# Two layers of attention on one core: the second attention's value products issued in bursts of four key blocks into a projection bank, with six score banks, three row slots, eight probability units and another order of the queues

## The reference, cut to what matters

```python
xn = _layernorm(x); x = x + L0_attn(xn) + L0_ffn(xn)     # 16 heads of 64, ALiBi slopes, causal
xn = _layernorm(x); x = x + L1_attn(xn) + L1_ffn(xn)     # 8 heads, differential, rotary

# L0_attn:  softmax(q k^T * SCALE + rel * slope, causal) @ v, then @ w_out + b_out
# L1_attn:  for each of 8 heads two score sets (q1,k1), (q2,k2) of width 8, no mask
o1 = sdpa(q1, k1, vfull); o2 = sdpa(q2, k2, vfull)       # vfull is 16 wide
o  = o1 - lam * o2
o  = o * rsqrt(mean(o*o) + EPS) * ln_w + ln_b
out = (o * (1 - LAMBDA_INIT)).reshape(b, s, e) @ Wo.T
# ffn:  z = silu(h @ w1 + b1) @ w2 + b2 ;  residual + 0.5 * z   (w1, w2 dequantised)
```

## Time and profile before

| | |
|---|---|
| three runs | 2512.21 us median (2510.09 to 2514.51) |
| the profiled execution's own time | 2513.58 us |
| its span, first to last instruction | 2511.6 us |
| TensorE busy / weight loads | 2370.6 us (94%) / 1112.7 us (44%) |
| DVE / ACT / POOL busy | 1856.1 (74%) / 1882.8 (75%) / 1430.7 us (57%) |
| mean granted TensorE clock | 0.986 |

### The profile page before, as it was taken

One profiled execution on the slowest core, in us unless ns is written; L12 is line 12 of the kernel. 1 busy time (PEld: TensorE's weight loads), 2 busy tenths in 40 slices (PEclk: granted clock), 3 DMA queues, 4 the chain that ended last, 5 costly groups with the idle time before them and its releaser, 6 DMA issues.

```text
span 2511.6 us, 81917 instructions
## 1 busy us (share of the span) xinstructions
PE 2370.6 (94%) x32896; PEld 1112.7 (44%) x32896; DVE 1856.1 (74%) x5637; ACT 1882.8 (75%) x4707; POOL 1430.7 (57%) x1356
## 2 busy tenths in 40 slices
PE   6999999999999999999999999999999999999886
PEld 2454444444444444444444444444444444444421
DVE  4558777777877778777777877778777776867675
ACT  4866787878778777787878778777787878778545
POOL 5866474665656556474665656556574655646311
PEclk8999999999999999999999999999999999999978
DMA  3002020200202002020200202002020200202020
GB/s 96 7 14 45 3 61 3 49 15 7 57 2 57 6 19 44 3 61 3 53 10 7 56 3 61 3 21 43 7 56 3 55 8 7 57 3 56 2 56 5
DMA packets 59944, 70.43 MB, mean 28 GB/s; under 512 B 11056, under 2 KB 55344, under 8 KB 56368
## 3 DMA queue, kind: packets, MB, share of 16 engines
q1 hardware_dynamic: 59568, 65.21, 11.5%
HBM read 35.04 MB, written 29.36 MB: 26 GB/s over the span
## 4 chain that ended last, share of the span: by engine, by line
PE 72%; ACT 14%; DVE 10%; issue 2%; DMA 1%; POOL 1%; SPq 0%; POOLq 0%; ACTq 0%; DVEq 0%
PE pj L1436 17%; PE pj L1532 10%; PE sc L1500 9%; PE op L1561 7%; PE sc L1517 7%; ACT pt L989 5%; PE pj L1548 5%; PE pj L1456 5%; DVE mx L1250 4%; PE sc L1605 4%; PE sc L1591 4%; ACT pq L949 3%; ACT pt L967 3%; PE pj L1426 3%; DVE pq L1197 2%
## 5 line engine op out<-in xcount | busy, mean ns | idle before, releaser
L818 POOL TENSOR_SCALAR pq<-pq,rsum 128x128 f32<-128x128 f32 (+3 forms) x1024 | 1130.5, 1121 | 743.0 <-DVE rsum L1204 742.6
L1250 DVE TENSOR_REDUCE mx<-sc 128x1 f32<-128x512 f32 x1024 | 655.9, 683 | 199.1 <-PE sc L1605 195.1
L989 ACT ACTIVATE pt<-sc 128x512 f32<-128x512 f32 x1024 | 556.3, 610 | 191.5 <-PE sc L1591 191.2
L949 ACT ACTIVATE pq<-pq,mx 128x128 f32<-128x128 f32 (+3 forms) x1024 | 573.2, 576 | 16.6 <-DVE mx L1197 16.6
L967 ACT ACTIVATE pt<-sc 128x512 f32<-128x512 f32 (+1 forms) x768 | 360.8, 538 | 221.2 <-PE sc L1517 217.7
L1197 DVE CUSTOM_DVE_ANT_0 pq<-sc,relkey 128x128 f32<-128x128 f32 (+3 forms) x1024 | 448.3, 484 | 104.9 <-PE sc L1500 100.0
L1500 PE MATMUL sc<-K,Q 64*128 64x128 f32 (+3 forms) x2048 | 365.5, 454 | 26.9 <-ACT pt L989 16.7
L1532 PE MATMUL pj<-pt,v 128*32 128x512 f32 (+3 forms) x4096 | 304.5, 438 | 3.9 <-ACT y L917 0.6
L1517 PEld LDWEIGHTS sc<-ident,pq 64*128 64x128 f32 x5120 | 199.2, 139 | 171.6 <-issue 127.3
L1436 PE MATMUL pj<-xnT,wqkv 128*32 128x512 f32 x2048 | 264.4, 609 | 7.6 <-DVE xres L1173 2.9
L1561 PE MATMUL op<-pt,v 128*32 128x512 f32 x1920 | 256.8, 607 | 2.2 <-ACT pt L989 2.0
(11 more groups left out here) (117 smaller groups left out, 2798.2 us busy)
## 6 DMA issues: line engine op xcount, KB each, us to landing
scr_p<-y SPq DMA_DIRECT2D x160, 128.0 KB, 2.4
QS<-scr_p SPq DMA_DIRECT2D x30, 384.0 KB, 6.1
KS<-scr_p SPq DMA_DIRECT2D x30, 384.0 KB, 8.8
x_in<-in_L_attn_x SPq DMA_DIRECT2D x16, 256.0 KB, 2.8
scr_p<-tanh SPq DMA_DIRECT2D x32, 128.0 KB, 2.4
out_x<-xres SPq DMA_DIRECT2D x15, 256.0 KB, 2.3
QS<-nrow SPq DMA_DIRECT2D x180, 4.0 KB
wqkv<-in_L_attn_w_qkv SPq DMA_DIRECT2D x1, 1536.0 KB, 6.5
```

What stands on the lines that cost most here:

```text
L818: pool.tensor_scalar(rows, rows, rsum[:, p % NROWS, c:c + 1], None, ALU.mult).then_inc(s_scl, 1)
L949: act.activation(rows, rows, ACT.Exp, scale=-1.0, bias=mx0[:, p % NROWS, c:c + 1], accum_out=lsum[:, p % NROWS, c:c + 1]).then_inc(s_exp0, 1)
L989: act.activation(pt1[:, GS * (m % 2) + 2 * j + h, :], sc[tile_bank(i, "st1", 2 * n + h)][:, :], ACT.Exp, scale=float(DS) ** -0.25).then_in ...
L1250: dve.reduce_max(mx1[:, g % 2, at:at + 1], sc[tile_bank(i, "mx1", 2 * t + h)][:, :], AXIS.X).then_inc(s_mxd1, 1)
```

## The change

It has five parts.

1. `pv1` is called once for a group instead of four times: 16 matmuls in a row, over the four key blocks, each block behind its own wait for the exponentials. Its result goes to a projection bank taken in turn (`w0` to `w3`), and `copy_heads` frees that bank. There are 4 calls to a sequence, in the step `VALUES_AT` (8 steps after the group's first key step).
2. The bank `op` becomes a sixth score bank (SCB = 6).
3. `pt1` holds eight units (a whole group) instead of four. `exp1` waits for the key block that used its unit last, which is a block of the group before.
4. `pq` has three slots of a pair instead of four; the last sequence's stacks, values and result lie in other slots, and wait for later pairs.
5. The order in all queues changes: the branches of `tick`, most of the tick constants, `score_order` and `pj_order`; DVE and ACT get branches of their own for the end.

```diff
-NROWS = 4
+NROWS = 3
+UNITS = 8
-PV_LAG = (0, 0)
-SCB = 5
+VALUES_AT = (8, 8)
+PJB = 2
+SCB = 6
-        pt1 = sb("pt1", [P, 2 * GS, T])
+        pt1 = sb("pt1", [P, 2 * UNITS, T])
-        op = ps("op")
             def copy_heads(i, g):
-                act.wait_ge(s_pv1, i.upto(NG * NT, NT * (g + 1)))
-                act.activation(oraw[:, :], op[:, :], ACT.Copy).then_inc(s_or, 1)
+                b, u = pj_use(i, f"w{g}")
+                act.wait_ge(s_pjf[b], u)
+                act.activation(oraw[:, :], pj[b][:, :], ACT.Copy).then_inc(s_pje[b], 1)
             def exp1(i, n):
-                m, j = divmod(n, GS // 2)
-                if j == 0:
-                    hold(act, s_pv1, i.upto(NG * NT, m - 1))
+                unit = i.upto(NU, n)
+                if unit >= UNITS:
+                    was, m = divmod((unit - UNITS) // (GS // 2), NG * NT)
+                    group, k = divmod(m, NT)
+                    if k < NT - 1:
+                        act.wait_ge(s_pv1, Seq(was).upto(NG * (NT - 1), (NT - 1) * group + k + 1))
+                    else:
+                        b, u = pj_use(Seq(was), f"w{group}")
+                        act.wait_ge(s_pjf[b], u)
-            def pv1(i, g, k):
+            def pv1(i, g):
+                t, full = bank(i, f"w{g}")
+                for k in range(NT):
+                    pe.wait_ge(s_exp1, i.upto(L1N, GS * (NT * g + k + 1)))
+                    for j in range(GS):
+                        unit = i.upto(NU, (GS * (NT * g + k) + j) // 2)
+                        last = pe.matmul(t[32 * j:32 * (j + 1), :], values1[i.last()][:, k, (GS * g + j) // 2, :],
+                                         pt1[:, 2 * (unit % UNITS) + j % 2, :], start=k == 0, stop=k == NT - 1)
+                    if k < NT - 1:
+                        last.then_inc(s_pv1, 1)
+                last.then_inc(full, 1)
...
-STORE_AT = (50, 56)
-STACK_AT = (58, 61)
+STORE_AT = (55, 55)
+STACK_AT = (56, 56)
...
```

More of the change, by code:

```diff
@@ L251, in l1_steps @@
             if i.live() and i.last() == (n == 1):
-                steps.extend((i, t) for t in l1_chunk(clock, part))
+                steps.extend((i, t) for t in l1_chunk(clock, n, part))
     return steps
@@ L284, in second, with values @@
                 order.append((f"n{group}", i.lo))
-            if (group := l1_heads(t, TURN_AT[i.last()])) is not None:
+            if (group := l1_heads(i, t, TURN_AT[i.last()])) is not None:
                 order.append((f"o{group}", i.lo))
+    def values(h, k, part):
+        for i, t in l1_steps(h, k, part):
+            if (group := l1_heads(i, t, VALUES_AT[i.last()])) is not None:
+                order.append((f"w{group}", i.lo))
     def pairs(name, g, lag):
@@ L1045, in tick @@
                         copy_q(i, p)
+                    p, i = pair(g, 1)
+                    if i is not None:
+                        exp0(i, p, 3)
                     p, i = pair(g, 2)
@@ L1063, in tick @@
                 elif r == 1:
-                    second_attention(h, k, 0)
+                    p, i = pair(g, 2)
+                    if i is not None:
+                        copy_turned(i, p, 5)
                     p, i = pair(g, 3)
@@ L1092, in tick @@
                     second_attention(h, k, 1)
-                    p, i = pair(g, 0)
-                    if i is not None:
-                        exp0(i, p, 3)
             pipeline(tick)
@@ L1359, in tick @@
                     prepare(g)
-                if r == 0:
-                    norms(g)
-                    others(g, h, k)
-                    second_attention(h, k, 0)
-                    p, i = pair(g, 1)
-                    if i is not None:
-                        invert_sums(i, p, 1)
+                if late(g) and r == 0:
                     p, i = pair(g, -1)
```

564 lines of the change are left out of this document (351 added, 213 removed).

## The result

The changed kernel takes 2478.08 us (median of 4 runs, 2476.94 to 2480.09), the kernel before 2511.15 beside it (4 runs, 2507.31 to 2514.51): a ratio of 0.987, 95% interval 0.9853 to 0.9887. The forecast was 2454 with a range of 2415 to 2500. The direction and the range were right, and 24 of the 57 us were missing. The profiled execution took 2480.09 us with a span of 2478.2.

A forecast was written before the change was run, and what follows sets the result against it. TensorE's own instruction stream was taken to set the time in the middle. From 2513.6 us, 43.7 for bursts, 10 for score banks and 5 for the end came off, giving 2454.9, forecast as 2454 us, range 2415 to 2500.

The forecast's parts named there:

- Bursts: On TensorE, batching the `pv1` calls saves 380 changes of shape at 0.115 us each, 43.7 us off.
- Score banks: Longer runs of score tiles take back what the sixth bank gives; 10 us off, bounds 50 off to 30 added.
- Rival 3: DVE and ACT starve during a burst and TensorE pays: slower, 2556 us, chance 0.09.
- rival 1: At the score banks, longer runs cost more than the sixth bank gives: 2494 us, chance 0.22.
- Calls' bank, units, row slots: Projection bank for calls, eight probability units and three row slots cost nothing; the bank's bound is 38 us.
- Moves on DVE, ACT and POOL: Row maxima and inverted sums move up one to two ticks ahead of POOL, free 62 us a sequence: nothing.
- The end: In the last sequence, keys issued ahead of the burst spare ACT waits: 5 us off, between 8 off and 10 added.
- What would show it: The list of signs in the traces by which the forecast was to be checked, mostly TensorE's times and waits.
- Distance of L1707: Sign in the middle: the time between two sequences falls from 151 to about 147.5 us.
- Idle near 5 us a sequence: Sign on TensorE: its idle time stays near 5 us a sequence; 7 or more would mean rival 1.
- Busy time 2330: Sign on TensorE: busy time falls by about 40 us to 2330, with as many matmuls.
- Wait of `exp1` for a call: Sign on ACT: its wait for the call stays below 1 us a time, costed at nothing.

The follow-up runs named there:

- y1: y0 with eight probability units and bursts, in the old order, with five score banks and the call's result still in `op`: 2629.49 us, ratio 1.0469.
- y2: y1 with the call's result in the projection banks' turn and six score banks, still in the old order: 2624.89 us, ratio 1.0451.
- x1: The changed kernel with five score banks and a bank of its own for the bursts' results, new order kept: 2692.64 us, ratio 1.0729.
- y0: The kernel before with three row slots in place of four and the last sequence's data in the changed kernel's places: 2510.56 us, ratio 0.999.
- x5: The changed kernel with ACT, DVE and POOL in the old order during the first sequence's first attention: 2488.12 us, ratio 0.9916.
- y3: y1 with the values of the last two sequences in single calls: 2608.15 us, ratio 1.0391.

## Why the prediction was right, and where not

The time lies in the stated range, 24 us from the likeliest value. Part of the agreement is luck: in the middle, effects of 7 to 13 us a sequence that the prediction put near nothing cancel, and ahead of the end two errors do.

- **Bursts, -43.7 us.** Size about right in the middle, mechanism right locally: 3.57 us for 32 records, 2.8 us a sequence by the rows, and the repeated sequence fell by 2.76. The calls' own rows give back 1.9 us in the changed kernel, in y1 and in y2, where 12 exits at 0.14 would give 1.7. But no run isolates the term in the time: where bursts alone were added, the sequence became longer by 6.7 us, so that the saved changes of shape explain nothing without the next two points. The busy time fell by 2.3 us a sequence (145.96 to 143.62), and by 14.5 in all, since the end added 18.
- **Score banks, -10 us, by "longer runs take back what the sixth bank gives".** Right as a net: the rows of the score banks fall by 0.3 us a sequence, 4 us in 13. The price of a tile beyond the banks was mis-sized. The bound took 0.33 us for it; x1 has 18 more of them than the changed kernel and is 13.3 us a sequence longer, 0.74 us each. The count is no rule by itself either: y2 with 26 is nearly as long as x1 with 38.
- **Rival 3, readers that starve in a burst.** Wrong for the change as a whole. In y1 and y2 its signs are there, but together with rival 1's longer runs, and the two are not separated. The argument against it (ACT has 33.7 us free a sequence) does not hold: in y1 ACT has 39.6 us free and TensorE still idles 5.6 us more. What keeps the loss off is the new order and the bank together, as y2 and x1 show: neither does it alone.
- **Calls' bank, units, row slots: nothing.** Row slots are confirmed by y0. The call's bank costs nothing in the new order; in the old one TensorE waits 41.7 us for its copy (y2), at another tile in the same bank, about the 38 us of the bound.
- **Moves on DVE, ACT and POOL: nothing.** This step failed. "POOL is free for 62 us a sequence" is a reading of the middle, and was carried to the start, where POOL is nearly full (33.6 of 40 us before, 36.4 after, from 60 to 100 us) and where x5 shows 10 us. The window of the start had been read too, with POOL at 88 of 125 us, and was not used.
- **The end, -5 us.** This step failed, with +20.5. It counted four bursts at up to 2.6 us and looked at the last group of the last sequence alone. There are eight bursts in the end, sequence 14's among them. With part of it at the lower clock, a burst's row takes 4.3 to 6.4 us in place of 3.64 (one of the eight takes 3.64), and one stands in front of a transpose on which the last sequence hangs. Ahead of the end, 54.0 us were won where bursts and banks were to bring 53.7, but that is two errors that cancel: 38.3 of them come from the repeated sequences, and 15.7 from a beginning that was costed at nothing. The whole miss shows in the end, 25.5 us, of which some 4 may be no more than the end of one execution differs from that of another (x5).
- **What would show it.** Distance of L1707 147.5: as said. Burst of 32 records in about 3.6 us: as said. Idle near 5 us a sequence: 3.9. Busy time 2330: 2356, a fall by a third of what was said. Wait of `exp1` for a call below 1 us: none to be seen.
- **A reading.** TensorE's row before has 36 full slices and not 37; nothing hangs on it.

## What to carry to other kernels

Batching one kind of work on the bound engine saves changes of shape (0.7 us for four calls here), and at the same time leaves its readers without tiles and joins the runs that its pieces had kept apart; which wins is settled by how many banks stand between and by what is queued behind the batch, so that the batch, the bank and the order should be costed together and not as a sum of edits. Read the beginning and the end of the program with their own windows, since an engine with 40% free in the middle can hold the others up there. In the end, look for the single chain that the last item hangs on, and let no long batch stand in its queue.

## What the runs showed of the hardware

TensorE's clock falls in the end although its row is busy: 147.82 of 185 us busy at a mean granted clock of 0.76 in the changed kernel, and 129.70 of 165 at 0.86 before. The granted clock there is 1.0 or 0.5 of full speed (2.4 or 1.2 GHz), for 88 us the lower. Four of the eight bursts, with their starts, show it in the duration of the same 32 matmuls; over the second row the clock was 1.00, over the third 0.56 in the mean, over the fourth 0.84:

```profile
2313.17 6.14 PE L1721 MATMUL pj<-pt,v 128*32 128x512 f32 x32
...
2336.89 3.64 PE L1721 MATMUL pj<-pt,v 128*32 128x512 f32 x32
...
2350.21 6.39 PE L1721 MATMUL pj<-pt,v 128*32 128x512 f32 x32
...
2460.23 4.29 PE L1721 MATMUL pj<-pt,pq 128*32 128x512 f32 x32
```

The one at 2350.21 follows the wait of 2.48 us above; ahead of the one at 2313.17 the trace shows only waits of 0.2 us. Which idle time brings the clock down is thus not settled here. y1 and y3 differ by 36 us of time at the lower clock in an end of the same matmuls (90 and 54 us). How much of the 21 us between them is the clock and how much the starved readers stays open.
